# Attention scores from two rounded fp32 parts on two halves of the array, with GpSimd splitting the row maxima

## The reference

```
q = (x @ WQ_w.T + WQ_b).reshape(b, s, NH, HD).transpose(0, 2, 1, 3)
k = (x @ WK_w.T + WK_b).reshape(b, s, NH, HD).transpose(0, 2, 1, 3)
v = (x @ WV_w.T + WV_b).reshape(b, s, NH, HD).transpose(0, 2, 1, 3)
scores = jnp.einsum('bhqd,bhkd->bhqk', q, k) * (1.0 / math.sqrt(HD))
scores = jnp.where(causal, -jnp.inf, scores)
attn = jax.nn.softmax(scores, axis=-1)
out = jnp.einsum('bhqk,bhkd->bhqd', attn, v)
```

## Time and profile before

| | |
|---|---|
| median of the runs | 950.53 us |
| span of the profiled execution | 947.1 us |
| busy: PE, DVE, ACT, POOL | 819.3, 620.1, 390.9, 149.4 us |
| L855, row maxima on DVE, each attention | 90.7 and 90.6 us in 152 instructions |
| L754 and L778, the two score products on PE, each attention | 58.0 and 46.6 us in 192 instructions each (at0) |
| L835, exponentials on ACT, each attention | 73.8 us in 96 instructions |

### The profile page before, as it was taken

The page is one execution under the profiler, slowest core; times in us unless marked ns, Lnnn a source line. Parts: engine busy times, 40 slices in busy tenths (PEclk is TensorE's granted clock), DMA queues, the critical chain, the costliest instruction groups (busy, mean ns, idle before and its releaser), DMA issues. The chain is left out here.

```text
span 947.1 us, 12745 instructions
## 1 busy us (share of the span) xinstructions
PE 819.3 (87%) x4477; PEld 508.3 (54%) x4477; DVE 620.1 (65%) x1318; ACT 390.9 (41%) x665; POOL 149.4 (16%) x205
## 2 busy tenths in 40 slices
PE   5556899997899897999997997778999999779896
PEld 3253343325688563344345796445556666447675
DVE  6887888826775688788636787453167671266774
ACT  3241456682621343566775433441122222133553
POOL 1500121130020001112310000104112221100143
PEclk9866899999999987899999998999999999989998
DMA  6326300000000454200006100894201110220000
GB/s 198 105 85 194 122 8 2 2 2 1 1 1 1 148 179 157 68 2 3 1 1 128 2 1 1 287 381 150 75 23 45 51 44 30 63 93 1 1 23 24
DMA packets 49557, 64.00 MB, mean 68 GB/s; under 512 B 12534, under 2 KB 34806, under 8 KB 49494
## 3 DMA queue, kind: packets, MB, share of 16 engines
q1 hardware_dynamic: 47302, 57.52, 19.7%
q0 software_dynamic: 1872, 5.13, 1.5%
q10 hardware_dynamic: 320, 0.52, 0.2%
HBM read 50.30 MB, written 15.51 MB: 69 GB/s over the span
## 5 line engine op out<-in xcount | busy, mean ns | idle before, releaser
L855 DVE TENSOR_REDUCE at1mx<-at1ps_s 128x1 f32<-128x512 f32 (+3 forms) x152 | 90.6, 656 | 19.9 <-PE at1ps_s L757 11.1
L855 DVE TENSOR_REDUCE at0mx<-at0ps_s 128x1 f32<-128x512 f32 (+3 forms) x152 | 90.7, 656 | 19.0 <-PE at0ps_s L757 11.1
L835 ACT ACTIVATE at1probs<-at1ps_e 128x1024 f32<-128x1024 f32 (+3 forms) x96 | 73.8, 809 | 47.9 <-PE at1ps_e L778 47.6
L835 ACT ACTIVATE at0probs<-at0ps_e 128x1024 f32<-128x1024 f32 (+3 forms) x96 | 73.8, 809 | 47.0 <-PE at0ps_e L778 46.7
L1137 PE MATMUL f2ps<-gu_raw,f2xT_b 128*128 x184 | 82.9, 593 | 1.0 <-ACT f2xT_b L1224 1.0
L1242 ACT ACTIVATE f2sg<-f2ps 128x512 f32<-128x512 f32 x30 | 17.8, 597 | 130.4 <-PE f2ps L1137 100.9
L754 PE MATMUL at0ps_s<-ks,qs 96*128 96x512 bf16 (+3 forms) x192 | 58.0, 364 | 5.1 <-DMA ks<-scratch 3.6
L754 PE MATMUL at1ps_s<-ks,qs 96*128 96x512 bf16 (+3 forms) x192 | 58.0, 361 | 2.5 <-DMA ks<-scratch 1.0
L1321 DVE TENSOR_TENSOR f2h<-f2sg,f2ps 128x512 f32<-128x512 f32 x30 | 20.5, 686 | 60.5 <-ACT f2sg L1242 29.0
L1137 PEld LDWEIGHTS f2ps<-gu_raw,f2xT_b 128*128 128x128 f32 x184 | 34.8, 190 | 35.5 <-issue 34.4
L778 PE MATMUL at1ps_e<-qs,ks 99*128 99x512 bf16 (+3 forms) x192 | 46.9, 341 | 5.3 <-DMA qs<-at1rows 3.4
(11 more groups left out here) (434 smaller groups left out, 1783.5 us busy)
## 6 DMA issues: line engine op xcount, KB each, us to landing
gu_raw<-in_L_ffn_w_gate_up SPq DMA_DIRECT2D x8, 1024.0 KB, 13.2
scratch<-parts SPq DMA_DIRECT2D x8, 768.0 KB, 3.9
qs<-scratch SPq DMA_DIRECT2D x48, 128.0 KB, 2.6
ks<-scratch SPq DMA_DIRECT2D x44, 128.0 KB, 2.7
dn_raw<-in_L_ffn_w_down SPq DMA_DIRECT2D x8, 512.0 KB, 12.3
f2x_in<-slots_in SPq DMA_DIRECT2D x23, 129.0 KB, 2.0
slots_in<-in_c_empty SPq DMA_DIRECT2D x1, 2944.0 KB, 18.8
traw<-in_L_ffn_w_gate_up SPq DMA_DIRECT2D x1, 2048.0 KB, 10.0
```

The lines of the kernel that those rows point to most:

```text
L835: act.activation(probs[:, slots(v), 0:n], ps_e[:, v % SCORE_PAIRS, :, 0:n], ACT.Exp, scale=HD ** -0.5)\
L855: dve.tensor_reduce(mx[:, p % 2, lo // CH, j:j + heads, t], rows_of, AX.X, ALU.max).then_inc(s_red, 1)
```

## The change

q and k become two parts each, rounded fp32 (fp32r, 4 bytes): three part pairs x 16 = 48 rows, and two rows for the maximum (50). Head j goes to lane j % 2: rows 0 to 63 or rows 64 to 127 of the stacks and of the array. The two heads of a pair are multiplied in the two halves. A maxima item holds heads of one lane. Bytes read back are the same (12 reads of 128 KB for each group), in rows of 4 KB in place of 2 KB; each write is 1 MB in place of 768 KB. In "s0" ScalarE still makes `whole`, and VectorE makes both parts; in "s1" ScalarE makes the first part and VectorE the second, straight from PSUM. VectorE's reduction yields negated maxima; GpSimd makes the two parts of the rows, in a list, PICKS, that mixes these splits with the zeroing; VectorE only merges the two key halves in every other phase. The planner's estimates are changed with it. Some buffers move (probabilities and rotary scratch into the room of the parts; a bias load becomes three DMAs instead of two).

```diff
-NSLOT = 6
+NSLOT = 3
 STK = NSLOT * HD
+LANES = 2
+LANE = P // LANES
 MP = 3
...
-PARTS_OF = ((0, 0, 0, 1, 1, 2), (0, 1, 2, 0, 1, 0))
+PARTS_OF = ((0, 0, 1), (0, 1, 0))
...
-def read_stack(eng, m, g, w, slots=range(NSLOT)):
-
-    for slot in slots:
+def read_stack(eng, m, g, w, pieces=range(LANES * NSLOT)):
+
+    for piece in pieces:
+        lane, slot = piece % LANES, piece // LANES
         part = PARTS_OF[w][slot]
-        src = m.scratch[w, part, g * GH * HD:(g + 1) * GH * HD, :].rearrange("(h d) n -> d h n", d=HD)
-        eng.dma_start(m.stacks[w][slot:STK:NSLOT, g, :, :], src).then_inc(m.stacked, 16)
-
-
-STACK_SIGNALS = 2 * NSLOT * 16
+        src = m.scratch[w, part, g * GH * HD:(g + 1) * GH * HD, :]\
+            .rearrange("(i l d) n -> l d i n", l=LANES, d=HD)[lane]
+        first = lane * LANE + slot
+        eng.dma_start(m.stacks[w][first:first + STK:NSLOT, g, :, :].bitcast(F32), src).then_inc(m.stacked, 16)
...
-            def middle(u):
-                act.wait_ge(rest_s, u + 1)
-                act.activation(part(u, 1), rest[:, u % 2, :], ACT.Copy).then_inc(mid, 1)
-
             for u, (f, w, c) in enumerate(UNITS):
                 act.wait_ge(full, u + 1)
-                if u >= 2:
-                    act.wait_ge(rest_s, u - 1)
-                act.activation(whole[:, u % 2, :], ps[:, u, :], ACT.Identity, bias=bias[:, w, f:f + 1],
-                               scale=1.0 if scale is None else scale[:, w, f:f + 1]).then_inc(whole_s, 1)
-                if u > 0:
-                    middle(u - 1)
-            middle(len(UNITS) - 1)
+                if scale is None:
+                    act.activation(part(u, 0), ps[:, u, :], ACT.Identity, bias=bias[:, w, f:f + 1]).then_inc(high, 1)
+                else:
+                    if u >= 2:
+                        act.wait_ge(low, u - 1)
+                    act.activation(whole[:, u % 2, :], ps[:, u, :], ACT.Identity, bias=bias[:, w, f:f + 1],
+                                   scale=scale[:, w, f:f + 1]).then_inc(whole_s, 1)
...
-            def third(u):
-                dve.wait_ge(mid, u + 1)
-                dve.tensor_tensor(part(u, 2), rest[:, u % 2, :], part(u, 1), ALU.subtract).then_inc(low, 1)
-
             for u, (f, w, c) in enumerate(UNITS):
-                dve.wait_ge(whole_s, u + 1)
-                dve.tensor_copy(part(u, 0), whole[:, u % 2, :]).then_inc(high, 1)
-                dve.wait_ge(high, u + 1)
-                if u >= 2:
-                    dve.wait_ge(low, u - 1)
-                dve.tensor_tensor(rest[:, u % 2, :], whole[:, u % 2, :], part(u, 0), ALU.subtract).then_inc(rest_s, 1)
-                if u > 0:
-                    third(u - 1)
-            third(len(UNITS) - 1)
+                if scale is None:
+                    dve.wait_ge(high, u + 1)
+                    dve.scalar_tensor_tensor(out=part(u, 1), in0=ps[:, u, :], scalar=bias[:, w, f:f + 1],
+                                             in1=part(u, 0).bitcast(F32), op0=ALU.add, op1=ALU.subtract).then_inc(low, 1)
+                else:
+                    dve.wait_ge(whole_s, u + 1)
+                    dve.tensor_copy(part(u, 0), whole[:, u % 2, :]).then_inc(high, 1)
+                    dve.wait_ge(high, u + 1)
+                    dve.tensor_tensor(part(u, 1), whole[:, u % 2, :], part(u, 0).bitcast(F32), ALU.subtract).then_inc(low, 1)
...
-        heads = CH // width
-        work += [(p, t, j, heads, PHASES[p][1] * CH, width) for j in range(0, GH, heads)]
+        if width * LANES <= CH:
+            work += [(p, t, tuple(range(lane, GH, LANES)), PHASES[p][1] * CH, width) for lane in range(LANES)]
+        else:
+            work += [(p, t, (j,), PHASES[p][1] * CH, width) for j in range(GH)]
...
-                for h in range(heads):
-                    a = h * width
-                    ins = pe.matmul(ps_s[:, i % MAX_BANKS, a:a + width], qs[0:STK, g, j + h, qt * P:qt * P + P],
-                                    ks[0:STK, g, j + h, lo:lo + width], start=True, stop=not last)
-                    if last:
-                        ins = pe.matmul(ps_s[:, i % MAX_BANKS, a + width - P:a + width], m.above[:], m.identb[:],
-                                        start=False, stop=True)
+                qt, last, lane = qc * TILES + t, lo == qc * CH, heads[0] % LANES
+                here = rows_of(lane, STK)
+                for h, j in enumerate(heads):
+                    ins = pe.matmul(ps_s[:, i % MAX_BANKS, h * width:(h + 1) * width], qs[here, g, j // LANES, qt * P:qt * P + P],
+                                    ks[here, g, j // LANES, lo:lo + width], start=(h == 0), stop=not last, skip_group_check=True)
+                if last:
+                    diagonal = ps_s[:, i % MAX_BANKS, 0:len(heads) * width].rearrange("p (h n) -> p h n", n=width)
+                    all_here = rows_of(lane, LANE)
+                    one = m.identb[all_here, lane * LANE:lane * LANE + LANE].unsqueeze(1).to_broadcast([LANE, len(heads), LANE])
+                    for other in range(LANES):
+                        a = width - P + (lane ^ other) * LANE
+                        ins = pe.matmul(diagonal[:, :, a:a + LANE], m.above[all_here, other, :], one,
+                                        start=False, stop=(other == LANES - 1), skip_group_check=True)
...
-                for i in range(PAIR):
-                    j = v % HALF * PAIR + i
-                    ins = pe.matmul(ps_e[:, v % SCORE_PAIRS, i, 0:n], ks[0:ROWS, g, j, kt * P:kt * P + P],
-                                    qs[0:ROWS, g, j, lo:lo + n], start=True, stop=True)
+                for lane in (first, 1 - first):
+                    here = rows_of(lane, ROWS)
+                    ins = pe.matmul(ps_e[:, v % SCORE_PAIRS, lane, 0:n], ks[here, g, v % HALF, kt * P:kt * P + P],
+                                    qs[here, g, v % HALF, lo:lo + n], start=True, stop=True)
...
+                c.step(pool.tensor_copy(high, least))
+                pool.tensor_tensor(low, least, high.bitcast(F32), ALU.subtract).then_inc(m_split, 1)
...
+            for kind, n in PICKS:
+                if kind == "select":
+                    select(n)
+                else:
+                    split_max(n)
...
+                dve.tensor_reduce(mx[:, p % 2, lo // CH, heads[0]:heads[-1] + 1:LANES, t], scored, AX.X, ALU.max,
+                                  negate=True).then_inc(s_red, 1)
...
-                if PHASES[p][1] == 0:
-                    c.step(dve.tensor_scalar(nm[:], mx[:, p % 2, 0], -1.0, None, ALU.mult))
-                else:
-                    c.step(dve.tensor_tensor(nm[:], mx[:, p % 2, 0], mx[:, p % 2, 1], ALU.max))
-                    c.step(dve.tensor_scalar(nm[:], nm[:], -1.0, None, ALU.mult))
-                c.step(dve.tensor_copy(high, nm[:]))
-                c.step(dve.tensor_tensor(rest[:], nm[:], high, ALU.subtract))
-                c.step(dve.tensor_copy(middle, rest[:]))
-                dve.tensor_tensor(low, rest[:], middle, ALU.subtract).then_inc(m_split, 1)
+                dve.tensor_tensor(nm[:, p // 2 % 2], mx[:, p % 2, 0], mx[:, p % 2, 1], ALU.min).then_inc(m_least, 1)
```

More of the change, by code:

```diff
@@ L889, in place @@
                 for j in range(GH):
[L890 to L891 removed]
+                    src = rows[j * MR * TILES:(j + 1) * MR * TILES, p % 2, :]
+                    first = j % LANES * LANE + STK
+                    sp.dma_start(qs[first:first + MR, g, j // LANES, qc * CH:qc * CH + CH].bitcast(F32), src)\
+                      .then_inc(placed[p % 2], 16)
             read_group(1)
```

255 lines of the change are left out of this document (151 added, 104 removed).

## The result

The change made the kernel slower: 995.37 us (median of 4, 991.06 to 997.47) against 950.4 us (4 runs, 949.87 to 951.98), ratio 1.0468 [1.0434, 1.0502]. The profiled execution took 991.06 us, span 988.9, mean granted clock 0.887 (before 950.53, 947.1, 0.942).

A forecast was written before the change was run, and what follows sets the result against it. TensorE bounds the kernel before, VectorE was to bound it after. Per attention 11.1 + 2.0 + 1.3 = 14.4 us, for two 28.8, take the span from 947.1 to 918.3; forecast 921 us, range 904 to 942.

The forecast's parts named there:

- the bound moves to VectorE: In VectorE's stretch of each attention, VectorE needs 94.0 us against TensorE's 69 to 90, so VectorE becomes the bound.
- TensorE's 78 to 94 us: TensorE's work per attention after the change: 78 us with everything paired, 94 with no maxima paired.
- TensorE stays the bound: First rival: loads pass singly, maxima rarely pair; 99 us of TensorE work per attention instead of 105; 936 us, chance 0.15.
- 110 with nothing paired: TensorE's work per attention if the halves don't run side by side; as a rival 965 us, chance 0.07.
- The load term: In TensorE's sum, a weight load in a stream costs at most 0.11 us; 192 score loads are 21 us.
- The rival that was under-weighted: the clock: Clock drops at phase starts in the attentions, 2.6 us each; one in every phase gives 964 us; chance 0.13, full or part.
- after 122 us the clock is 1.00 throughout: Argument against the clock rival, from at0's windows in the kernel before.
- the forecast gain of 11.1: VectorE's stretch of reductions in each attention falls from 113.1 to 102.0 us, a gain of 7.2 to 19.1.
- The end, 2.0 forecast: Each attention's end, after the last reduction, gets 2.0 us shorter (0 to 3).
- A split with its merge is some 1.0 us long: Cost of GpSimd's split of a phase's maxima in the attentions, no later than before.
- The start, 1.3 forecast: Stages s0 and s1 ahead of each attention gain 1.3 us in the mean (-1.5 to 2.2).
- Moved buffers at nothing: Moved buffers, one more bias DMA and wider mask conversion, ahead of the first layer's norm stage, cost nothing; otherwise 0.76 us.

The follow-up runs named there:

- e14: e9 with VectorE's reductions reading half of their columns and exponentials and zeroing done for one head of a pair: 956.28 us.
- e9: e8 with maxima and score products on all 64 rows of a half, the rows between zeroed by four DMAs per layer: 990.88 us.
- e1: Kernel before with maxima products on 48 of 96 rows and score products on 35 of 99: 1092.72 us.
- e12: e9 with VectorE's reductions reading half of their columns: 980.57 us.
- e5: Kernel before with maxima and score products on rows 0:66 instead of 0:96 and 0:99: 985.19 us.
- e11: Kernel before with maxima products alone on 66 of their 96 rows: 960.83 us.
- e7: Kernel after plus a 64-row, 512-column bf16 product only where two maxima items follow each other, 116 per attention: 985.43 us.
- e3: Kernel after plus a bf16 product of 64 rows by 512 columns ahead of each maxima item, 160 per attention: 987.66 us.
- e15: e9 with exponentials and zeroing for one head of a pair, and the other head's score products left out: 986.41 us.
- e8: Kernel after with VectorE's last residual addition waiting for GpSimd's last split: 986.78 us.
- e6: Kernel before with negated reductions, three bf16 parts and the splits of the maxima on GpSimd, TensorE's order unchanged: 950.17 us.

## Why the prediction was wrong

It said 921 us (904 to 942), faster with 0.85; the time is 995, beyond every rival.

**The step that failed: "the bound moves to VectorE".** VectorE's need was right (93.5 us of reductions and 0.7 of merges, against 94.0), TensorE's 78 to 94 us was not: it is 107 (e14). The halves run side by side in the array, as taken from the column quarters, but the order puts lone pairs and single items between whole-array products, and there a pair costs what two products cost in a row (0.43 us in e9). The rival that "TensorE stays the bound" allowed 99 us; the top of that sum, 110 with nothing paired, was nearest, and it stood with 0.07. The load term (0.11 us at most, from a stream of whole-array products) could not show the price of changing between half and whole, since the trace of before has no product on half of the rows. It has a hint, unread: a single product ahead of a values step, which works on column quarters, takes 0.31 us where one in a stream takes 0.21. e1 shows that price with bf16 weights, so the fp32r load is not needed for it; how the 0.43 us of a lone fp32r pair divides between load and change of form stays open. The Trainium skill, TensorEngine Tiling (Array Packing), section PSUM Bottleneck, names the copying out of PSUM as what may become the bottleneck; here it is not, for with half of VectorE's reading a group lost 0.9 of 29.3 us (e12).

**The rival that was under-weighted: the clock.** That "after 122 us the clock is 1.00 throughout" was no evidence: those rows were made by products on 96 and 99 rows. The changed kernel's are on 48 and 50. e5 and e11 show that fewer rows alone, in the same order and form, lower the clock and cost 32 and 10 us. The mechanism given, drops at phase starts where VectorE paces TensorE, has a part too as far as e7 shows it (10 us back), but its price of 2.6 us for a drop was too small: in the third group one lasts from about 153 to 163.5 us and slows values and scores with it. How much is rows and how much pacing can't be divided: e3 and e9 bring 1.00 back in at0 in two ways, e9's at1 stands at 0.94 in its last groups, and e15 falls with 64 rows. What sets the clock stays open beyond this.

**Sizes.** Groups two to four of at0 take 94.8 us (116.18 to 210.95), before 86.8. Three groups at e9's 29.3 would be 87.8, so some 1 us is structure and 7 the clock, give or take what e8 shows of the scatter. The first group adds 5.3 us, at 0.50 throughout. By this estimate the forecast gain of 11.1 never was there to be had: without any clock loss the stretch would have been no shorter than before. So the step that failed took the gain away, and the clock made most of the loss.

**The end, 2.0 forecast, -3.6 measured.** "A split with its merge is some 1.0 us long" held seven times in eight; the last one met the addition to x, 1.9 us of cast (e8 gives back 2.7 in all). The rest goes with the clock, 0.82 there.

**The start, 1.3 forecast, -1.8 and -0.5 measured.** The 2.2 us earlier write came as said (4.2 after the start of s0, 6.5 before). The term that was mis-sized is the write of 1 MB: 6.35 us to the reads, not 5.0. From the first q read to the first reduction it is 12.55 us, before 11.1: the twelve reads, of the same 128 KB each, did not "cost what they cost" (from issue to landing 3.2 and 3.6 us for q and k in the median, before 2.6 and 2.7).

**Moved buffers at nothing.** The start of s0 came 4.5 us later here, but over the runs it scatters: 56.6 to 58.3 us in five profiles on the kernel before, 57.7 to 61.5 in twelve on the kernel after. It goes with how long TensorE runs at half speed at the program's start. In the kernel before the rotary stage's products are fast from the first one on (first line); in the kernel after they take twice as long until about 24 us (the other two):

```profile
13.46 1.10 PE L321 MATMUL rotps<-wa,xT 128*128 128x256 f32 x4 [2.17 <-PEq L119]
...
14.31 2.04 PE L325 MATMUL rotps<-wa,xT 128*128 128x256 f32 x4 [2.17 <-PEq L122]
...
24.15 1.13 PE L325 MATMUL rotps<-wa,xT 128*128 128x256 f32 x4
```

Where these products come up to speed at the same point, about 17 us from the start, s0 starts at the same time as well: at 57.85 us in e6 and 58.07 in e1 on the kernel before, at 57.81 in e7 and 58.06 in e9 on the kernel after. So "nothing" held as far as these rows show, and the 4.5 us go with the clock of this one execution.

**The sum itself.** Its ends do not use the ends of its own terms: 2 x (7.2 + 0 - 1.5) = 11.4 and 2 x (19.1 + 3 + 2.2) = 48.6 give 939 and 902, not 936 and 908. And the seven splits are 7.5 us, not 8.0, for the four without a merge hold the reductions up for 0.93 each. Neither comes near 995.

**Not tried:** an order that gathers half-array products and whole-array products into longer runs, which the readings point to, and whether the clock follows the values as well as the rows. No version here beats the kernel before; e6 equals it.

## What to carry to other kernels

Splitting TensorE's array pays for streams of small products (four in 0.46 us here). Where such products alternate one by one with whole-array ones, each change cost 0.1 to 0.2 us here, and a lone pair as much as two products; count places in the order, not columns. And before taking work from a busy TensorE, ask what the clock has been earned with: a kernel that stands at 1.00 may lose it by using fewer rows (e5, e11), and then everything on the engine gets slower. An engine that is relieved (VectorE in e6 and e12) gives little or nothing while another one holds the group. And look where a total hides an experiment's own cost: e9's zeroing DMAs took back what its rows had gained.
